# Maxima products of an attention kernel taken from the placed tiles, in the full tile shape, one head behind the other

## The chip, the cores and the metric

The kernel runs on one core of a Trainium2 chip. The metric is the device time of one execution, in microseconds (us). The kernel before takes 3608.76 us (median of three runs, 3608.7 to 3609.93 us). Engines are called by their profile names: PE (TensorE), PEld (its weight loads), DVE (VectorE), ACT (ScalarE), POOL (GpSimd), and SP (SyncE), which here only issues DMA transfers; SPq is its queue in the rows.

## The reference, cut to what matters

The input is x of shape (8, 1024, 256). After a layer norm, the result is x + attention(xn) + mixture-of-experts(xn). The attention has 16 heads of width 64:

```
q = xn @ Wq.T + bq ; k = xn @ Wk.T + bk ; v = xn @ Wv.T + bv      (8 batches, 16 heads, 1024, 64)
att = softmax(q @ k.T / 8)                                         (1024 x 1024 for each batch and head)
out = (att @ v) @ Wo.T + bo
```

The experts (64 of width 192, 8 chosen for each token) take their turns beside the attention. All is computed to float32 accuracy. Where a product runs in the one-pass format of float32 (`F32R`), its operands are split into a rounded "high" part and a "low" rest, and products of the parts are added up.

## The kernel before, in words

Four stages follow one another: layer norm and values (`norm_stage`), a small table of token counts (`table_stage`), attention together with experts (`attention_stage`), and the output projection (`output_stage`). The change is in the third.

The attention stage works on pairs of heads: 8 batches by 8 pairs make NP = 64 pairs. `run_steps` runs steps s = -2 to 64. In step s the kernel finishes pair s-1 (`fin`), computes scores, exponentials and values products of pair s (`att`), computes the maxima of pair s+1 (`nxt`), projects queries and keys of pair s+2 (`prj`), and works on one expert. Steps 3 to 60 are a hardware loop, two steps an iteration; the others are written out.

**How a pair moves through the tiles.** The projection (`PJ`, L974) leaves queries and keys in PSUM. ACT writes their rounded high part into `high` (L1033), DVE the rest into `low` (L1107). In both tiles the two heads of a pair lie on partitions 0 to 63 and 64 to 127. Scores want another layout, so SP copies them, from SBUF to SBUF, with 12 transfers a pair (`SHUFFLES`), which are called the placement here: for each head, `k_full` holds the high keys twice (top and bottom 64 partitions), `q_full` the high queries on top of the low queries, `k_rest` the low keys, and `q_rest` the high queries. They increment the semaphore `placed` (16 each, 192 a pair). In step s SP issues the placement of pair s+1 once three things have come about: all four low parts of that pair (`lows_ready`), the placement before, and the last exponential of step s-1 (`probs_ready`, since the buffers to be overwritten were read by the scores of that pair). On SP's queue the placement stands behind the store of the second half's output of step s-1 (`store`, L1269) and the load of half of the projection's input for a later pair (`load_tokens`, L777, 1 MB); behind it come the row of maxima (L1261), the next expert's weights (L1301 to L1306), the next values (L1315), projection weights, the other half of the input, and stores.

**Scores.** `score` writes keys by queries of one head, 128 by 512, into one of three PSUM banks, with two matmuls (L898 with 128 rows of `k_full` and `q_full`, L901 with 65 rows of `k_rest` and `q_rest`; the 65th row subtracts each query's maximum). The step's first score waits for `placed` of its own pair. ACT turns them into exponentials (L1062), POOL adds these up (L1226, L1227), PE multiplies them with the values (`pv`, L942), and `add_up` (L952) sums over keys.

**Maxima.** `quad` computes, for 128 queries of the pair s+1, both heads' products with all 1024 keys, in four PSUM banks of 512 columns (`work`): four matmuls of 64 rows each (L927), straight from `high`. They go part by part, and within a part head 0 (rows 0 to 63), then head 1 (rows 64 to 127). DVE reduces each head's two banks to a negated maximum (L1099). Each step has 8 quads. The wait at the step's first quad, `highs_ready`, is for the pair's high parts, which ACT wrote in the step before.

**The order on PE.** It is written out by hand in `step` and is the same for each of four slots g: eight scores, with a projection and an expert's or transpose's item between them; quad 2g; in slot 0 `add_up(s, 1)` and the last `pv` of pair s-1, in slot 2 `add_up(s, 0)`, in slots 1 to 3 `pv(s, g-1)`; quad 2g+1. An engine does its instructions in order, so whatever stands behind a waiting instruction waits too.

Of the kernel before, what the change touches and what calls it, by code (L numbers as in the profile page):

```python
# [25 lines left out]
P = 128  # L26
B, N, D = 8, 1024, 256
T = B * N
H, DK = 16, 64
# [11 lines left out]
HALF = 512  # L41
# [5 lines left out]
DMA = 16  # L47
# [12 lines left out]
def known(v, least):  # L60

    return isinstance(v, int) and v < least
# [628 lines left out]
SHUFFLES = 12  # L691
# [97 lines left out]
def attention_stage(nc, ctx, io, keep):  # L789
    def sb(name, shape, dt=F32):  # L790
        return ctx.enter_context(nc.sbuf_tensor(name, shape, dt))

    def sem(name):
        return ctx.enter_context(nc.semaphore(name))
# [5 lines left out]
    work = psum[:, 4:8, :]  # L800
# [3 lines left out]
    q_full = sb("q_full", [P, 2, 2, N], F32R)  # L804
    q_rest = sb("q_rest", [DK + 1, 2, 2, 2, HALF], F32R)
    k_full = sb("k_full", [P, 2, 2, N], F32R)
    k_rest = sb("k_rest", [DK + 1, 2, 2, N], F32R)

    high = sb("high", [P, 2, 2, N], F32R)
# [32 lines left out]
    highs_ready = sem("highs_ready")  # L842
    lows_ready = sem("lows_ready")
    placed = sem("placed")
    quad_filled = sem("quad_filled")
# [33 lines left out]
    def _(pe):  # L879
# [24 lines left out]
        def quad(s, par, flags, q):  # L904

            g = q // 2
            fin, att, nxt, prj = flags
            if q == 0:
                pe.wait_ge(highs_ready, 4 * (s + 2))
            if q % 2 == 0:  # L910
                if prj:
                    pe.wait_ge(lows_ready, 4 * (s + 2) + g + 1)
                if att and g == 0:
                    pe.wait_ge(xt_copied, s + 1)
                    pe.wait_ge(shift_ready[1], s + 1)
                if att and g == 1:
                    pe.wait_ge(gate_ready, s + 1)
                if g == 2:
                    pe.wait_ge(shift_ready[0], s + 2)
                if att and g == 3:  # L920
                    pe.wait_ge(y_weighted, s + 1)
            if not known(QUADS * (s + 1) + 2 * q, 1):
                pe.wait_ge(quad_reduced, QUADS * (s + 1) + 2 * q)
            for part in range(2):
                for h in range(2):
                    rows = slice(DK * h, DK * (h + 1))
                    last = nc.tensor.matmul(work[:, 2 * h + part, :], high[rows, 1 - par, 0, q * P:(q + 1) * P],  # L927
                                            high[rows, 1 - par, 1, part * HALF:(part + 1) * HALF], start=True, stop=True)
                    if part == 1:
                        last.then_inc(quad_filled, 1)  # L930

        def pv(p, par, gg):
            pe.wait_ge(probs_ready, SCORES * p + 8 * (gg + 1))
# [69 lines left out]
        def step(s, par, flags):  # L1003
            fin, att, nxt, prj = flags
            for g in range(SLOTS):
                for n in range(2 * GROUP):
                    if att:
                        score(s, par, fin, g, n // 2, n % 2)
                    if n in ITEMS[g] and present(ITEMS[g][n], g, flags):
                        item(s, par, flags, g, ITEMS[g][n])  # L1010
                if nxt:
                    quad(s, par, flags, 2 * g)
                if g == 0 and fin:
                    add_up(s, 1, fin)
                    pv(s - 1, 1 - par, SLOTS - 1)
                if g == 2 and att:
                    add_up(s, 0, fin)
                if g > 0 and att:
                    pv(s, par, g - 1)
                if nxt:  # L1020
                    quad(s, par, flags, 2 * g + 1)
# [610 lines left out]
```

## Time and profile before

| | |
|---|---|
| median of three runs | 3608.76 us |
| the profiled execution | 3610.97 us |
| its span, first to last instruction | 3609.2 us |
| mean granted PE clock | 0.984 of full |
| PE busy | 3503.0 us, 97% |
| POOL busy | 2711.3 us, 75% |
| DVE busy | 2517.0 us, 70% |
| ACT busy | 1685.6 us, 47% |
| maxima products, L927 | 2048 matmuls, 378.0 us busy |

The span is divided by stage: up to about 408 us lie the first two stages, then the attention stage up to about 3395 us, then the output stage. Busy times are of the whole span; a group of instructions by line shows its summed time without overlaps and the mean length of one, which is longer where two run at once.

### The profile page before, as it was taken

The page shows a single profiled execution, that of the slowest core. Times are in us where ns is not written, and L with a number is a line of the kernel's source. Part 1 is how long each engine was busy: PE and PEld are TensorE (multiplying, and loading weights), DVE is VectorE, ACT ScalarE, POOL GpSimd, SP SyncE. Part 2 cuts the span into 40 slices and gives each one's busy share as a digit, 9 for nine tenths or more (in the row PEclk, how much of TensorE's full clock was granted, in tenths as well). Part 3 has the DMA queues.
Part 4 walks back from the last instruction along what each step waited for, and adds up shares of the span by engine and source line. Part 5 has one row for each costly group of instructions (what it writes and reads, how often), then busy time and mean ns, then how long its engine had stood idle before and what let it go on. Part 6 is the DMA issues. An engine that isn't in the chain of part 4 may idle for free. (4 is left out here: it accounts for less than half of the span.)

```text
span 3609.2 us, 59812 instructions
## 1 busy us (share of the span) xinstructions
PE 3503.0 (97%) x16231; PEld 2104.9 (58%) x16232; DVE 2517.0 (70%) x3256; ACT 1685.6 (47%) x3126; POOL 2711.3 (75%) x2338
## 2 busy tenths in 40 slices
PE   8999489999999999999999999999999999999899
PEld 6888255555555555555555555555555555555487
DVE  7888467777777777777777777777777777777444
ACT  4455234444444444444444444444444444444343
POOL 1111168888888888888888889888888888889511
PEclk9999689999999999999999999999999999999899
DMA  7777545666666666666666666666666666665396
GB/s 249 230 227 224 150 117 137 173 168 168 169 168 170 170 168 168 170 171 169 170 169 172 168 169 169 171 167 171 168 171 168 168 169 172 169 172 130 117 320 227
DMA packets 393627, 635.53 MB, mean 176 GB/s; under 512 B 48048, under 2 KB 214640, under 8 KB 393584
## 3 DMA queue, kind: packets, MB, share of 16 engines
q1 hardware_dynamic: 370800, 603.54, 60.3%
q0 software_dynamic: 14336, 23.08, 3.1%
q10 hardware_dynamic: 8448, 8.39, 0.7%
q8 instruction: 21, 0.34, 0.0%
q14 instruction: 22, 0.18, 0.0%
HBM read 306.91 MB, written 126.12 MB: 120 GB/s over the span
## 5 line engine op out<-in xcount | busy, mean ns | idle before, releaser
L1099 DVE TENSOR_REDUCE merged<-psum 128x1 f32<-128x1024 f32 x1024 | 1206.0, 1219 | 732.9 <-PE psum L927 726.8
L1062 ACT ACTIVATE probs<-psum 128x512 f32<-128x512 f32 x2048 | 1083.3, 600 | 1160.5 <-PE psum L901 867.6
L1226 POOL TENSOR_TENSOR sums<-sums,probs 128x512 f32<-128x512 f32 x768 | 979.8, 1276 | 97.9 <-ACT probs L1062 43.4
L1227 POOL TENSOR_TENSOR sums<-sums,probs 128x512 f32<-128x512 f32 x768 | 981.1, 1277 | 0.0
L942 PE MATMUL psum<-probs,v_sb 128*64 128x512 f32 x4096 | 931.0, 596 | 0.0
L898 PE MATMUL psum<-q_full,k_full 128*128 128x512 f32 x2048 | 878.8, 429 | 0.0
L901 PE MATMUL psum<-q_rest,k_rest 65*128 65x512 f32 x2048 | 812.3, 397 | 0.0
L942 PEld LDWEIGHTS psum<-probs,v_sb 128*64 128x64 f32 x4096 | 284.0, 137 | 560.8 <-issue 498.4
L898 PEld LDWEIGHTS psum<-q_full,k_full 128*128 128x128 f32 x2048 | 388.2, 190 | 196.9 <-issue 95.2
L1127 DVE RECIPROCAL sum_all<-sum_all 128x128 f32<-128x128 f32 x512 | 448.7, 918 | 27.7 <-ACT sum_all L1070 27.7
L974 PE MATMUL psum<-x_t,w_qk 128*128 128x512 f32 x1536 | 416.3, 407 | 38.0 <-DVE w_d L1092 27.5
L901 PEld LDWEIGHTS psum<-q_rest,k_rest 65*128 65x128 f32 x2048 | 390.0, 190 | 61.5
L927 PE MATMUL psum<-high 64*128 64x512 f32 x2048 | 378.0, 446 | 18.9 <-DVE merged L1099 12.2
L974 PEld LDWEIGHTS psum<-x_t,w_qk 128*128 128x128 f32 x1536 | 282.2, 193 | 135.0 <-DVE w_d L1092 27.7
L927 PEld LDWEIGHTS psum<-high 64*128 64x128 f32 x2048 | 154.4, 186 | 324.1 <-issue 299.5
L1226 POOL TENSOR_TENSOR sums<-probs 128x512 f32<-128x512 f32 x128 | 165.5, 1293 | 174.9 <-ACT probs L1062 173.2
L1033 ACT ACTIVATE high<-psum,bias 128x512 fp32r<-128x512 f32 x256 | 176.0, 688 | 238.0 <-PE psum L974 233.2
L1107 DVE SCALAR_TENSOR_TENSOR low<-psum,bias,high 128x512 fp32r<-128x512 f32 x256 | 177.4, 693 | 28.1 <-ACT high L1033 28.1
L1527 PE MATMUL psum<-ot_sb,wo 128*128 128x512 f32 x768 | 186.7, 402 | 10.3 <-ACT ot_sb L1447 10.3
L1527 PEld LDWEIGHTS psum<-ot_sb,wo 128*128 128x128 f32 x768 | 145.7, 192 | 45.7 <-issue 11.2
L1422 POOL TENSOR_TENSOR rest<-x_out,moe_sb 128x1024 f32<-128x1024 f32 x16 | 41.2, 2575 | 165.1 <-DVE y L1484 129.7
L1227 POOL TENSOR_TENSOR sums<-probs 128x512 f32<-128x512 f32 x128 | 163.0, 1274 | 0.0
(145 smaller groups left out, 3059.8 us busy)
## 6 DMA issues: line engine op xcount, KB each, us to landing
x_t<-xt SPq DMA_DIRECT2D x118, 1024.0 KB
k_full<-high SPq DMA_DIRECT2D x256, 256.0 KB
v<-values SPq DMA_DIRECT2D x64, 512.0 KB, 3.2
w_qk<-wqk_parts SPq DMA_DIRECT2D x64, 512.0 KB
q_full<-high SPq DMA_DIRECT2D x128, 256.0 KB
q_full<-low SPq DMA_DIRECT2D x128, 256.0 KB
k_rest<-low SPq DMA_DIRECT2D x128, 256.0 KB
q_rest<-high SPq DMA_DIRECT2D x128, 256.0 KB
```

What stands on the lines that cost most here:

```text
L898: nc.tensor.matmul(out, k_full[:, par, h, keys], q_full[:, par, h, cols], start=True, stop=False)
L901: nc.tensor.matmul(out, k_rest[:, par, h, keys], q_rest[:, par, half, h, :], start=False, stop=True).then_inc(scores_ready, 1)
L927: last = nc.tensor.matmul(work[:, 2 * h + part, :], high[rows, 1 - par, 0, q * P:(q + 1) * P], high[rows, 1 - par, 1, part * HALF:(part + ...
L942: last = nc.tensor.matmul(out_ps[rows, :], v_sb[:, par, kt, rows], probs[:, kt, h, :], start=(kt == 0), stop=(kt == KT - 1))
L974: last = nc.tensor.matmul(out, w_qk[:, par, which, wp, kd, :], x_t[:, xp, kd, cols], start=(j == 0 and kd == 0), stop=(j == 2 and kd == KD ...
L1062: nc.scalar.activation(probs[:, kt, h, :], ring[ring_place(g, j) % RING], ACT.Exp, scale=SCALE).then_inc(probs_ready, 1)
L1099: nc.vector.tensor_reduce(out=merged[:, col:col + 1], in_=work[:, 2 * h:2 * h + 2, :].rearrange("p b c -> p (b c)"), axis=AX, op=ALU.max, ...
L1107: nc.vector.scalar_tensor_tensor(out=low[:, par, which, cols], in0=work[:, 0, :], scalar=bias[:, par, which:which + 1], in1=f32(high[:, pa ...
L1127: nc.vector.reciprocal(sum_all[:, half, cols], sum_all[:, half, cols]).then_inc(recip_ready, 1)
L1226: nc.gpsimd.tensor_tensor(sums[:, half, 0, :], first[:, 0, :], probs[:, kt, 0, :], ALU.add)
L1227: nc.gpsimd.tensor_tensor(sums[:, half, 1, :], first[:, 1, :], probs[:, kt, 1, :], ALU.add).then_inc(sums_added, 1)
L1527: last = nc.tensor.matmul(psum[:, 2 * par + c, :], wo[:, t, h, c * P:(c + 1) * P], ot[:, par, o, h, :], start=(n == 0), stop=(n == 3 * PAI ...
```

## The change

Two edits, both in `quad`:

```diff
             if q == 0:
-                pe.wait_ge(highs_ready, 4 * (s + 2))
+                pe.wait_ge(placed, DMA * SHUFFLES * (s + 2))
...
-            for part in range(2):
-                for h in range(2):
-                    rows = slice(DK * h, DK * (h + 1))
-                    last = nc.tensor.matmul(work[:, 2 * h + part, :], high[rows, 1 - par, 0, q * P:(q + 1) * P],
-                                            high[rows, 1 - par, 1, part * HALF:(part + 1) * HALF], start=True, stop=True)
-                    if part == 1:
-                        last.then_inc(quad_filled, 1)
+            for h in range(2):
+                for part in range(2):
+                    last = nc.tensor.matmul(work[:, 2 * h + part, :], q_full[:, 1 - par, h, q * P:(q + 1) * P],
+                                            k_full[:, 1 - par, h, part * HALF:(part + 1) * HALF], start=True, stop=True)
+                last.then_inc(quad_filled, 1)
```

The four products of a quad read `q_full` and `k_full`, 128 rows each, in place of 64 rows of `high`; a product is then (high + low queries) by high keys. Head 0's two parts come first, then head 1's, and DVE is told of a head after its second matmul: after matmuls 2 and 4, where it was after 3 and 4. The first quad of step s waits for the placement of pair s+1, which SP issues in the same step, in place of the high parts that were ready in the step before.

## Rows read from the trace of the kernel before

**Rows 1.** The page: busy us of each engine, share of the span, instructions
```profile
PE 3503.0 (97%) x16231; PEld 2104.9 (58%) x16232; DVE 2517.0 (70%) x3256; ACT 1685.6 (47%) x3126; POOL 2711.3 (75%) x2338
```
**Rows 2.** Windows of the loop's stage: length, each engine's busy us (instructions), clock, DMA share, GB/s
```profile
524.00:3300.00 2776.00, 2775.53 (x12894) 1553.00 (x12889) 1978.05 (x2313) 1334.59 (x2612) 2465.20 (x2129) 1.00 0.64 168
```
**Rows 3.** Timeline of PE, one step: start, us, instruction, count; quad 0 first and last
```profile
1799.25 0.73 PE L927 MATMUL psum<-high 64*128 64x512 f32 x4
...
1844.91 0.73 PE L927 MATMUL psum<-high 64*128 64x512 f32 x4
```
**Rows 4.** Timeline of PE, a quad between a score and pv, and scores behind another
```profile
1811.37 0.40 PE L901 MATMUL psum<-q_rest,k_rest 65*128 65x512 f32 x1
1811.70 0.73 PE L927 MATMUL psum<-high 64*128 64x512 f32 x4
1812.37 3.65 PE L942 MATMUL psum<-probs,v_sb 128*64 128x512 f32 x16
...
1816.61 0.50 PE L898 MATMUL psum<-q_full,k_full 128*128 128x512 f32 x1
1816.95 0.40 PE L901 MATMUL psum<-q_rest,k_rest 65*128 65x512 f32 x1
1817.19 0.40 PE L898 MATMUL psum<-q_full,k_full 128*128 128x512 f32 x1
```
**Rows 5.** Waits in the whole span: who for whom, us in total, times, longest
```profile
DVE merged L1099 <- PE psum L927: 726.8, 506, 3.4
```
**Rows 6.** Timeline of ACT: the last two exponentials of a step
```profile
1833.85 1.08 ACT L1062 ACTIVATE probs<-psum 128x512 f32<-128x512 f32 x2
```
**Rows 7.** Timeline of SP in that step: issues of the input, the placement, the weights
```profile
1834.13 0.62 SPq L777 DMA_DIRECT2D x_t<-xt  x1
1835.03 1.17 SPq L1289 DMA_DIRECT2D k_full<-high  x2
...
1849.33 1.28 SPq L1290 DMA_DIRECT2D q_rest<-high  x1
...
1851.77 0.40 SPq L1301 DMA_DIRECT2D w_gu<-in_w_gu  x1
```
**Rows 8.** Window over the placement's transfers, columns as in rows 2
```profile
1836.00:1855.00 19.00, 19.00 (x90) 10.63 (x87) 12.84 (x15) 8.42 (x17) 17.07 (x15) 1.00 1.04 238
```
**Rows 9.** DMA issues, 1834 to 1860 us: KB each, us from issue to landing
```profile
w_gu<-in_w_gu SPq DMA_DIRECT2D x1, 384.0 KB, 5.0
```
**Rows 10.** DMA issues, 1800 to 1900 us: a store of 256 KB
```profile
ot<-out_raw SPq DMA_DIRECT2D x4, 256.0 KB, 2.0
```
**Rows 11.** Timeline of PE at the stage's head, with the idle time before and its releaser
```profile
430.94 1.22 PE L927 MATMUL psum<-high 64*128 64x512 f32 x4 [1.66 <-DVE low L1107]
...
437.20 2.90 PE L974 MATMUL psum<-x_t,w_qk 128*128 128x512 f32 x6 [1.40 <-DVE merged L1099]
...
477.57 0.84 PE L927 MATMUL psum<-high 64*128 64x512 f32 x4 [2.41 <-DVE merged L1099]
...
478.94 0.63 PE L901 MATMUL psum<-q_rest,k_rest 65*128 65x512 f32 x1
```
**Rows 12.** Windows of 0.5 us there: PE busy (instructions), clock, DMA share, GB/s
```profile
440.50:441.00 0.50, 0.00 (x0) 0.99 0.84 172
...
478.00:478.50 0.50, 0.50 (x5) 0.56 0.76 169
...
484.50:485.00 0.50, 0.50 (x3) 0.61 0.00 0
```
**Rows 13.** SP at the head and in step 1: first issue of a placement without an input load
```profile
426.39 1.18 SPq L1289 DMA_DIRECT2D k_full<-high  x2
...
511.12 1.16 SPq L1289 DMA_DIRECT2D k_full<-high  x2
```
**Rows 14.** Window of 2 us in the head's placement, columns as in rows 2
```profile
430.00:432.00 2.00, 1.06 (x4) 0.53 (x4) 0.75 (x1) 0.01 (x1) 0.00 (x0) 0.50 0.99 201
```
**Rows 15.** Timeline of PE, quad 0 of step 1
```profile
520.98 0.73 PE L927 MATMUL psum<-high 64*128 64x512 f32 x4
```

## The prediction

> **What bounds the kernel now.** Read the page first: PE is busy for 97% of the span, POOL for 75, DVE for 70 [rows 1]. Shares of a whole span mix stages, so the next view is the window over the attention loop: 2775.53 of 2776.00 us of PE are busy, at the full granted clock [rows 2]. There PE is the bound without a gap, and a step takes what its instructions take: quad 0 starts at 1799.25 and again at 1844.91, 45.66 us later [rows 3]. Everything else has slack; DVE waits 726.8 us for the maxima products, 1.4 us a time [rows 5]. So whatever is added to PE's order, as work or as a wait, goes into the time in full, 64 times (steps -1 to 62 have quads), and what DVE gains does not.
>
> **The wait.** In the step of the rows, the last score's exponential ends at 1833.85 + 1.08 = 1834.93 [rows 6]. SP issues 1 MB of input at 1834.13, then, from 1835.03 on, the 12 placement transfers; the last goes out at 1849.33 and is issued by 1850.61 [rows 7]. PE reaches quad 0 at 1844.91 [rows 3]. Even the issuing ends 5.7 us behind it, so the new wait stalls PE in every step, and the price is set by the landing. No row has that landing; it is bounded from both sides.
> - From below: a 256 KB store on a quiet queue lands 2.0 us after its issue [rows 10]; from 1850.61 that gives 1852.6.
> - From above: the expert's weights, issued at 1851.77 right behind, land 5.0 us later [rows 7, 9]; the same lag from 1850.61 gives 1855.6.
> - By bytes: 19 us at 238 GB/s from 1836 to 1855 are 4.52 MB [rows 8]. The input (1.05), twelve times 0.262 (3.15) and POOL's gather and scatter (0.20) make 4.39 MB, so the placement ends close to 1855. The weights say the same: landed at 1856.8, and 0.39 MB at this rate take 1.6 us, so they begin at 1855.1.
>
> I take 1855.0, since two ways meet there. PE would come to quad 0 not at 1844.91 but 0.4 us later (quads 6 and 7, which lie between the last exponential's scores and quad 0, get dearer, below). The stall is 1855.0 - 1845.3 = 9.7 us; by the bounds 7.3 to 10.3.
>
> Does it recur in full? Yes: the placement starts at the last exponential of the step before, and from there to quad 0 PE's path is fixed, so the distance is the same each time; time lost behind quad 0 delays the next exponential and with it the next placement. What is queued behind quad 0 on PE is `add_up`, the last `pv` of the pair before, and all scores; ACT, DVE and POOL stand behind these, so nothing is done in the stall that would be saved later. On SP the next values' load waits for that `pv`, and now goes out after it, about when it would anyway, a step before its use: nothing. The DMA engines are full during the placement (share 1.04 in rows 8), so it can't be expected to shorten.
>
> **The matmuls.** Now a quad lasts from its start to the next instruction 1812.37 - 1811.70 = 0.67 us for four matmuls [rows 4]. Full-shape matmuls of 512 columns follow one another at 1817.19 - 1816.95 = 0.24 us. But the shape changes cost something now: from the score to the quad 1811.37 to 1811.70 = 0.33, and the first score behind a quad takes 1816.61 to 1816.95 = 0.34, each 0.10 over the 0.24. A full-shape quad with `pv` on one side and scores on the other: 4 x 0.24 = 0.96 for 0.67, less one border of 0.10, so +0.2 us. Bounds: none of the border comes back, +0.3; both borders come back, +0.1. There are 8 quads a step, of which two hide in the stall (subtracted there): 8 x 0.2 = 1.6 us (0.8 to 2.4). The earlier signal for head 0 (after matmul 2) is worth nothing while DVE waits for PE; the second is later by the 0.3 us of the quad, under DVE's mean wait of 1.4 us.
>
> The Trainium skill bears on this ("TensorEngine Tiling (Array Packing)", Key Properties): a change of tiling mode drains TensorE, while differing tiles compute in parallel. The first half speaks for the change, the second against it. The borders of 0.33 and 0.34 us and the two overlapping matmuls of a pair show both; by the drain alone the edit would gain 0.1 us a quad, and with the parallelism lost it costs 0.2.
>
> **The clock.** The stall has a second price. At the stage's head PE idles 2.41 us before 477.57; at 478.0 to 478.5 the granted clock falls to half (1.2 GHz), and full (2.4) is back at about 484.7 [rows 11, 12]. The score matmul at 478.94 takes 0.63 us there, where the same one takes 0.40 at full clock [rows 11, 4]. Four times in the head PE came to work with the clock already at half; in three of them full clock returned 3.3 us after the start of the work (as 437.20 to 440.5, rows 11 and 12), in the fourth later, but within 6 us. A stall of 9.7 us is longer than any of those gaps, so PE will come out of it at half clock, for 3.3 to 6.6 us (440.5 - 437.20 and 484.7 - 478.1); half of that is lost: 1.6 to 3.3 us. I take 2.5, the middle. With no drop it would be 0.
>
> The skill's "TensorE: Matmul & The Clock Gate", HAM oscillation, tells of this pattern: a loop whose iterations each wait on a DMA pays the return to full clock every time. The rows at the head agree in kind (1.2 GHz after idling 2.41 us); whether it comes back in this loop no row of before can show.
>
> **Sum.** A step of the loop: 9.7 + 1.6 + 2.5 = 13.8 us. Input loads precede the placement in steps 4 to 61, 58 steps: 800 us. In steps 1, 2, 3 and 62 there is no such load. The placement alone is 3.15 MB at 0.2 MB/us [rows 14], 15.7 us, with 0.9 us beside the data (2.0 us for the store of rows 10, less 0.262 MB at the 0.238 of rows 8): in step 1, 511.12 + 16.6 = 527.7, against quad 0 at 520.98 + 0.4 [rows 13, 15], a stall of 6.3; with 1.6 and 2.5 that is 10.4 us, four times 42 us. Step -1: 426.39 + 16.6 = 443.0 against 430.94 [rows 11, 13], 12.1 us, and 1.5 for dearer quads at half clock: 14. Step 0: its placement waits for low parts and not for exponentials; by the same reckoning about 4.5 of stall, 1.6 and 1.5 more: 8. Together 800 + 42 + 22 = 864 us. The profiled execution took 3610.97 us, 1.8 us over its span, 2.2 us over the median. 3610.97 + 864 = 4475; in terms of the median, **4473 us**. A step of the loop would last 59.5 us.
>
> **The rivals.**
> 1. *The stall comes, the clock stays.* Then 64 x 2.5 = 160 us less: 4313. For it: the fall at 478 came in one particular head, with sparse work before. Against: the clock also fell to half in the head's other gaps, all shorter than 9.7 us.
> 2. *The clock recovers late.* If, instead of 3.3 to 6.6, some 12 us go at half clock in each step, 3.5 us more are lost: +224, 4697. For it: a step that stalls regularly has less activity than any stretch of the loop before. Against: after every gap in the head it was full again within 7.2 us of the work's start.
> 3. *The wait is hidden, only the matmuls count.* 512 quads at 0.2: +102, 3711. It wants the placement landed by 1845.3, 10 us after its first issue. Against: SP issues until 1850.61.
> 4. *Not slower: the full shape gains.* One mechanism: no change of shape around quads any more. If a full-shape quad cost no more than the 0.67 us of now, the two borders would give back 0.2 us x 512 = 102 us: 3507. It decides only if the 64-row pairs do not really run side by side (four matmuls spaced 0.24 would fall to 0.17), and if the landing comes before PE is at quad 0. The rows of scores at 0.24 and rows 7 are against both.
> 5. *The edit does not do what it says*: were `placed` already at its count at quad 0, because the counts refer to an earlier pair. Then the time would be rival 3's. They don't: 192 x (s+2) is pair s+1's, the one issued in this step.
>
> **From there to the numbers.** The forecast 0.84, rival 1 0.06, rival 2 0.04, rival 3 0.03, rival 4 0.01 and the rest 0.02 (among it no change). The forecast's own ends: a step of 7.3 + 0.8 + 1.6 = 9.7 to 10.3 + 2.4 + 3.3 = 16.0 us, so +610 to +1010 us; the low end needs three extremes at once. The range reaches from 4290, which takes in rival 1, to 4620. A difference of 0.2% (7 us) is about what a measurement of this kernel can tell; slower by more than that has 0.97, within it 0.01, faster 0.02.
>
> **What would show it right or wrong.** In the profile after: PE's share falls to about 83% (49.8 of 59.5 us in a step), with an idle time of about 9.7 us ahead of the first matmul of quad 0 in each step, released by a DMA or unexplained; quad 0 to quad 0 59.5 us; a granted clock of 0.50 for some us behind it, and a mean over the loop of about 0.90 (5 us of work and some 6 of the stall at half, of 59.5); L927 at 0.24 us from matmul to matmul. Steps of 47 us without gaps would mean the placement had landed; steps of 57 with the clock at 1.00, rival 1; steps over 62, rival 2 or a placement that got slower.

## The result and the profile after

| | before | after |
|---|---|---|
| median | 3608.78 us (4 runs) | 4554.1 us (4 runs, 4548.15 to 4558.06) |
| ratio, 95% interval | | 1.2617 [1.2595, 1.2639] |
| profiled execution, span | 3610.97, 3609.2 us | 4558.06, 4556.3 us |
| mean granted PE clock | 0.984 | 0.902 |
| L927 (L926 after), PE busy | 378.0 us | 663.0 us |

The change costs 945 us, where 864 were forecast. Lines behind `quad` stand two lower after the change, in `quad` one. The page's busy times answer to [rows 1], the window over the loop to [rows 2]:

```profile
PE 3806.6 (84%) x16232; PEld 2387.3 (52%) x16232; DVE 2534.6 (56%) x3256; ACT 1685.6 (37%) x3126; POOL 2710.8 (59%) x2338
```
```profile
524.00:4300.00 3776.00, 3142.22 (x13207) 1865.27 (x13206) 2047.19 (x2366) 1369.68 (x2682) 2530.59 (x2186) 0.90 0.49 125
```

PE was busy without a gap in this stage; now 634 of its 3776 us are idle, and the clock is 0.90. The busy time of ACT and POOL is what it was, that of DVE 18 us more in 2517: the other engines have hardly more work. The waits (who for whom, us in total, times, longest) name the reason; the DVE row answers to [rows 5]:

```profile
PE psum L926 <- DMA q_rest<-high: 651.5, 64, 14.7
DVE merged L1097 <- PE psum L926: 1580.1, 512, 14.4
```

64 waits, one for each step with quads, all released by the last transfer of the placement. They make up 651.5 of the 945 us. One of them, in SP's timeline, which answers to [rows 7]:

```profile
1978.04 0.62 SPq L777 DMA_DIRECT2D x_t<-xt  x1
1979.52 1.16 SPq L1287 DMA_DIRECT2D k_full<-high  x2
...
1993.08 1.29 SPq L1288 DMA_DIRECT2D q_rest<-high  x1
```

and in PE's, quad 0 first, then `add_up`, `pv` and quad 1 (idle time and its releaser in brackets):

```profile
1999.33 2.05 PE L926 MATMUL psum<-k_full,q_full 128*128 128x512 f32 x4 [9.69 <-DMA q_rest<-high]
2001.31 1.98 PE L950 MATMUL psum<-sums,ones 128*64 128x512 f32 x4
2003.07 4.86 PE L940 MATMUL psum<-probs,v_sb 128*64 128x512 f32 x16
2007.86 1.20 PE L926 MATMUL psum<-k_full,q_full 128*128 128x512 f32 x4
```

The last transfer is issued by 1994.37 and lands 5.0 us later. The reader should also see what follows the wait: `add_up` takes 2003.07 - 2001.31 = 1.76 us to the next line. The same three pieces in slot 2 of the step before, without a wait in front:

```profile
1965.62 1.08 PE L926 MATMUL psum<-k_full,q_full 128*128 128x512 f32 x4
1966.64 1.08 PE L950 MATMUL psum<-sums,ones 128*64 128x512 f32 x4
1967.55 3.60 PE L940 MATMUL psum<-probs,v_sb 128*64 128x512 f32 x16
1971.08 1.20 PE L926 MATMUL psum<-k_full,q_full 128*128 128x512 f32 x4
```

From quad to next quad 8.53 us behind the wait, 5.46 without: 3.07 us are lost to the clock in this step (2.65 in the next). These two lie above the mean: over all 61 waits of the loop it is 7.86 us from quad 0 to quad 1 (6.90 to 8.59), where 5.54 pass at full clock (so in `e3_shape_only`, below), so 2.3 us a step. Windows of 1 us show it (PE busy, clock, DMA share, GB/s), as [rows 12] did at the head: the clock falls at 1992, in the wait, and is full again at 2005.5, 6 us after the work has started.

```profile
1990.00:1991.00 1.00, 0.00 (x0) 1.00 1.04 252
1992.00:1993.00 1.00, 0.00 (x0) 0.50 1.02 225
1999.00:2000.00 1.00, 0.67 (x2) 0.50 0.64 213
2004.00:2005.00 1.00, 1.00 (x6) 0.50 0.00 0
2005.00:2006.00 1.00, 1.00 (x4) 0.70 0.00 0
2006.00:2007.00 1.00, 1.00 (x8) 1.00 0.00 0
```

The quads themselves, between a score and `pv`, and between `pv` and scores; these answer to [rows 4]:

```profile
1977.88 0.39 PE L901 MATMUL psum<-q_rest,k_rest 65*128 65x512 f32 x1
1978.28 1.18 PE L926 MATMUL psum<-k_full,q_full 128*128 128x512 f32 x4
1979.39 3.65 PE L940 MATMUL psum<-probs,v_sb 128*64 128x512 f32 x16
1982.98 1.20 PE L926 MATMUL psum<-k_full,q_full 128*128 128x512 f32 x4
1984.01 0.39 PE L898 MATMUL psum<-q_full,k_full 128*128 128x512 f32 x1
1984.24 0.40 PE L901 MATMUL psum<-q_rest,k_rest 65*128 65x512 f32 x1
```

From score to `pv` it is now 1.51 us for 1.00 before: the border in front stayed (0.40), and four matmuls take 1.11 for 0.67. That first border is not the same at every quad. In slot 2, where `add_up` follows, it is gone (1965.62 - 1965.39 = 0.23 us, before 0.33):

```profile
1965.39 0.39 PE L901 MATMUL psum<-q_rest,k_rest 65*128 65x512 f32 x1
```

In front of the quads that `pv` follows, it varies from 0.24 to 0.44 us. From quad to the second matmul of the scores, 1.26 for 1.00: four take 1.03, and the 0.10 of the border behind them is gone (0.23).

The loop's step, from quad 0 to quad 0 over 54 steps, is (4191.05 - 903.84)/54 = 60.9 us, against 45.66 before [rows 3]; the forecast had 59.5:

```profile
903.84 2.05 PE L926 MATMUL psum<-k_full,q_full 128*128 128x512 f32 x4 [9.68 <-DMA q_rest<-high]
```
```profile
4191.05 2.07 PE L926 MATMUL psum<-k_full,q_full 128*128 128x512 f32 x4 [9.55 <-DMA q_rest<-high]
```

### The profile page after: what moved, and what is told of

It reads as the page before. It is cut to its first block and busy times, and to the rows that moved or that the text cites. A ratio compares the mean times of both kernels' runs of the same rounds, so it can differ in the third digit from the quotient of the medians.

```text
span 4556.3 us, 59813 instructions
## 1 busy us (share of the span) xinstructions
PE 3806.6 (84%) x16232; PEld 2387.3 (52%) x16232; DVE 2534.6 (56%) x3256; ACT 1685.6 (37%) x3126; POOL 2710.8 (59%) x2338
## 5 line engine op out<-in xcount | busy, mean ns | idle before, releaser
L926 PE MATMUL psum<-k_full,q_full 128*128 128x512 f32 x2048 | 663.0, 449 | 666.0 <-DMA q_rest<-high 651.5
L940 PE MATMUL psum<-probs,v_sb 128*64 128x512 f32 x4096 | 969.9, 617 | 0.0
L926 PEld LDWEIGHTS psum<-k_full,q_full 128*128 128x128 f32 x2048 | 384.5, 206 | 1004.1 <-issue 871.2
L898 PE MATMUL psum<-q_full,k_full 128*128 128x512 f32 x2048 | 851.3, 416 | 0.0
L940 PEld LDWEIGHTS psum<-probs,v_sb 128*64 128x64 f32 x4096 | 298.4, 145 | 627.3 <-issue 580.9
L1068 ACT COPY sum_all<-psum 128x512 f32<-128x512 f32 x128 | 74.9, 585 | 920.8 <-PE psum L950 920.8
L972 PEld LDWEIGHTS psum<-x_t,w_qk 128*128 128x128 f32 x1536 | 294.6, 192 | 109.0 <-DVE w_d L1090 27.6
L1224 POOL TENSOR_TENSOR sums<-probs 128x512 f32<-128x512 f32 x128 | 164.7, 1287 | 220.0 <-ACT probs L1060 213.2
L1105 DVE SCALAR_TENSOR_TENSOR low<-psum,bias,high 128x512 fp32r<-128x512 f32 x256 | 189.6, 741 | 27.4 <-ACT high L1031 27.4
L950 PE MATMUL psum<-sums,ones 128*64 128x512 f32 x512 | 190.6, 833 | 3.6 <-POOL sums L1225 3.6
```

The lines of the kernel that those rows point to most:

```text
L898: nc.tensor.matmul(out, k_full[:, par, h, keys], q_full[:, par, h, cols], start=True, stop=False)
L926: last = nc.tensor.matmul(work[:, 2 * h + part, :], q_full[:, 1 - par, h, q * P:(q + 1) * P], k_full[:, 1 - par, h, part * HALF:(part + 1) ...
L940: last = nc.tensor.matmul(out_ps[rows, :], v_sb[:, par, kt, rows], probs[:, kt, h, :], start=(kt == 0), stop=(kt == KT - 1))
L950: last = nc.tensor.matmul(ring[place % RING][DK * h:DK * (h + 1), :], ones[:], sums[:, half, h, :], start=True, stop=True)
L972: last = nc.tensor.matmul(out, w_qk[:, par, which, wp, kd, :], x_t[:, xp, kd, cols], start=(j == 0 and kd == 0), stop=(j == 2 and kd == KD ...
L1224: nc.gpsimd.tensor_tensor(sums[:, half, 0, :], first[:, 0, :], probs[:, kt, 0, :], ALU.add)
```

## The experiments

**The wait alone** (`e1_wait_only`), from the kernel before:

```diff
             if q == 0:
-                pe.wait_ge(highs_ready, 4 * (s + 2))
+                pe.wait_ge(placed, DMA * SHUFFLES * (s + 2))
```

> The kernel before with the new wait alone: the first quad of a step waits for its pair's placement, the products stay the 64-row pairs from the high parts. My theory: the wait is nearly all of the loss. In the changed kernel a step waits 10.2 us in the mean and loses about 2.9 us to the half clock; here quads 0 to 5, which lie behind the wait, are each 0.25 to 0.5 us shorter (1.85 us a step), and quads 6 and 7, which lie in front of it, only lengthen the wait by 0.7 us. So 4554 - 64 x 1.85 = about 4436 us, stalls of about 11 us in each step. Rival (the dearer products and the change of shapes around them are what costs, the wait is partly made up elsewhere): under 4100 us.

Measured: 4448.64 us, 1.2325 [1.2301, 1.2349] of before. PE's waits, and the products at their old cost:

```profile
PE psum L927 <- DMA q_rest<-high: 697.8, 64, 14.9
```

The wait brings 840 of the 945 us: 698 as idle time, the other 142 (2.2 us a step) with the clock, whose mean over the loop is 0.90 here too. From quad 0 to quad 1 it is 7.28 us here in the mean of the loop, for 5.10 before: the same 2.2. The idle time is 46 us longer than after the whole change, 0.7 us a step; there two dearer quads stand ahead of the wait, and by the lines above they cost 0.51 and 0.26 us more.

**The products alone** (`e3_shape_only`), with the old wait, and for that reason from other data: 128 rows of the high parts, so a product is the sum over both heads. The edit against the changed kernel, beside the old wait:

```diff
             for h in range(2):
                 for part in range(2):
-                    last = nc.tensor.matmul(work[:, 2 * h + part, :], q_full[:, 1 - par, h, q * P:(q + 1) * P],
-                                            k_full[:, 1 - par, h, part * HALF:(part + 1) * HALF], start=True, stop=True)
+                    last = nc.tensor.matmul(work[:, 2 * h + part, :], high[:, 1 - par, 0, q * P:(q + 1) * P],
+                                            high[:, 1 - par, 1, part * HALF:(part + 1) * HALF], start=True, stop=True)
```

> The kernel before with full-shape products, one head behind the other, but read from the high parts (128 rows of both heads, so each product is the sum over both heads; the maxima are of that sum) and with the old wait. Theory: the products' share of the change by itself, 8 quads a step with 0.25 us more each in front of scores and 0.5 us more in front of values products: 512 x 0.33 = 170 us, 3780 us, PE busy without a gap and the clock full. By the forecast's term (0.2 us a quad) it would be 3711 us. Rival (no changes of shape around quads, hence no loss): 3609 us or less.

Measured: 3759.3 us, 1.0419 [1.0398, 1.0439]; PE busy for 2774.29 us of the window of 2776 and the clock full. 151 us over 512 quads are 0.295 us each; a step of the loop takes 48.14 us for 45.66, 0.31 a quad. The two halves of the change add up to 840 + 151 = 991; less the 46 us that are hidden in the wait, that is the 945.

**The order alone** (`e2_order_only`): the 64-row products as before, head 0's two first.

```diff
-            for part in range(2):
-                for h in range(2):
+            for h in range(2):
+                for part in range(2):
...
-                    if part == 1:
-                        last.then_inc(quad_filled, 1)
+                last.then_inc(quad_filled, 1)
```

> The kernel before with the order of the four products alone: head 0's two parts, then head 1's, still 64 rows each from the high parts, old wait. Theory (products on different row halves run side by side, so order matters as much as shape): matmuls on the same rows follow one another at about 0.24 us, a quad takes 0.95 to 1.05 instead of 0.67 us, and the time is 3609 + 512 x 0.3 = about 3770 us. Rival (only the full shape costs, order is free, or the earlier signal to the reducing engine helps): 3605 to 3620 us.

Measured: 3608.42 us, 1.0001 [0.999, 1.0011]. My theory fell: order costs nothing. A quad between `pv` and scores:

```profile
1847.29 0.74 PE L927 MATMUL psum<-high 64*128 64x512 f32 x4
1847.96 0.50 PE L898 MATMUL psum<-q_full,k_full 128*128 128x512 f32 x1
```

It still takes 0.67 us. So either 64 rows are fast by themselves, or the pairs form whatever the order. The next two ask that.

**One half of the rows** (`e8_same_rows`): all four products from rows 0 to 63.

```diff
-                    rows = slice(DK * h, DK * (h + 1))
+                    rows = slice(0, DK)
```

> The kernel before with all four 64-row products of a quad read from rows 0 to 63 (the second head's maxima are then the first head's), same order and wait. e2_order_only took no time, which fits two readings. Theory (the halves of the rows work side by side, and in e2 the second head's products were started beside the first head's although they stand behind them): with one half only, four products go one behind the other at 0.235 us, a quad takes 0.95 to 1.0 us, and the time is 3609 + 512 x 0.3 = about 3760 us, as e3_shape_only. Rival (64 rows are fast by themselves, the other half has nothing to do with it): 3605 to 3615 us.

Measured: 3828.55 us, 1.0612 [1.0591, 1.0633]:

```profile
1824.95 1.20 PE L927 MATMUL psum<-high 64*128 64x512 f32 x4
1826.07 0.50 PE L898 MATMUL psum<-q_full,k_full 128*128 128x512 f32 x1
1826.41 0.39 PE L901 MATMUL psum<-q_rest,k_rest 65*128 65x512 f32 x1
```

A quad takes 1.12 us for 0.67, and here both borders stay as well (0.34 behind it). The rival is out: the saving of the kernel before lies in the two halves working side by side. The starts in the traces say so directly. In the kernel before, the four products of this kind of quad start at 0, 0.003, 0.337 and 0.340 us, so two at a time; in this run one by one, 0.23 to 0.34 us apart. 220 us over 512 quads are 0.43 each; I had expected 0.3, the figure of the full shape, which gets rid of one border. Four 64-row products on one half are dearer than four of 128 rows.

**A fence between the heads** (`e9_order_fenced`): e2 with a wait, long met, in front of head 1's first product.

```diff
             for h in range(2):
+                if h:
+                    pe.wait_ge(lows_ready, 4 * (s + 2))
                 for part in range(2):
```

> e2_order_only with a wait that has long been met between the first head's two products and the second head's. Theory (in e2 a product of the second head is started ahead of one of the first head on its own half of the rows): if the wait holds the second head back until the queue reaches it, the first head's two products go one behind the other, a quad takes about 0.95 us, and the time is about 3740 to 3770 us. Rival (the start order has nothing to do with the queue's order or was changed when the program was compiled, and such a wait stops nothing): 3605 to 3620 us.

Measured: 3607.98 us, 0.9999 [0.9989, 1.0009]. It stops nothing. The records of the trace show what runs: the product that carries this wait, head 1's first, starts 0.007 us behind head 0's first, and head 0's second only 0.33 us later, although it stands ahead in the kernel. In e2, too, the two that start last are the ones that signal DVE, one of each head. So between products on different halves of the rows, the order of starts is not that of the kernel. Whether head 1's product overtakes on the engine or was put in pairs when the program was compiled is left open.

**The engine kept at work** (`e4_warm`): the changed kernel with the old wait first, 36 matmuls whose result quad 0 overwrites, and then the new wait.

```diff
+            if q == 0:
+                for _ in range(36):
+                    nc.tensor.matmul(work[:, 0, :], high[:, 1 - par, 0, 0:P], high[:, 1 - par, 1, 0:HALF],
+                                     start=True, stop=True)
+                pe.wait_ge(placed, DMA * SHUFFLES * (s + 2))
```

> The changed kernel with 36 more full-shape matmuls ahead of the wait for the placement in each step, on data that is ready, their result overwritten by quad 0. They take 36 x 0.236 = 8.5 us of a stall of 10.2 us, so PE works through it. Theory (the half clock behind the stall is a cost of its own, 2.9 us a step): the clock stays full, the step loses only the wait, 4554 - 64 x 2.9 = about 4370 us. Rival (the clock's fall costs nothing, since the matmuls behind it wait for something else): 4554 us; if the stall has more to do with contention by PE's reads, more than 4554 us.

Measured: 4426.97 us, 1.2271 [1.2247, 1.2295] of before, 127 us under the changed kernel, with 36 matmuls more a step. A stall:

```profile
1707.60 8.43 PE L926 MATMUL psum<-high 128*128 128x512 f32 x36
1717.58 1.19 PE L931 MATMUL psum<-k_full,q_full 128*128 128x512 f32 x4 [1.56 <-DMA q_rest<-high]
1718.70 1.08 PE L955 MATMUL psum<-sums,ones 128*64 128x512 f32 x4
```

Quad 0 is at 1.12 us again, and the clock of the loop is 0.99 for 0.90. Useless work makes the kernel faster. The gain is 2.0 us a step, not the 2.9 that I had taken from two steps: the mean loss is 2.3 (above), and some of it is left here, since PE still idles for 1.8 us in the mean of the loop and then needs 5.98 us from quad 0 to quad 1, for 5.54 at full clock.

**Less in front of the landing.** `e5_split` sends the eight transfers into `k_full` and `q_full` first, with a semaphore of their own for which the quads wait; `e6_late` loads the input's second half behind the next step's placement; `e7_split_late` does both.

```diff
-                pe.wait_ge(placed, DMA * SHUFFLES * (s + 2))
+                pe.wait_ge(placed_full, DMA * FULLS * (s + 2))
...
-                        sp.dma_start(f32(dst[to, pp, h, :]), f32(src[rows, pp, which, :])).then_inc(placed, DMA)
+                        sp.dma_start(f32(dst[to, pp, h, :]), f32(src[rows, pp, which, :])).then_inc(placed_full, DMA)
```
```diff
-            if loads:
-                alone(sp, (standing, 1), (lows_ready, 4 * (s + 2) + 4), (x_loaded[1], DMA * x_loads(s + 2)))
-                load_tokens(sp, io, keep, s + 3, 1)
...
+            if not known(s, LOOP0) and not (isinstance(s, int) and s > NP - 3):
+                alone(sp, (standing, 1), (lows_ready, 4 * (s + 1) + 4), (x_loaded[1], DMA * late_loads(s + 1)))
+                sp.dma_start(...)     # input of pair s+2, second half
```

> The changed kernel with the placement reordered and its signal divided: the eight transfers into the two tiles that the quads read go first and have a semaphore of their own, the quads wait for these only; the four others follow. Theory (the landing is a matter of bytes in front of it: 1.05 MB of input and 3.15 MB of placement at 0.2 to 0.24 MB a us): 1.05 MB less, the wait shrinks by 4.4 to 5.2 us to some 5.5 us; the clock still falls. 4554 - 64 x 4.8 = about 4250 us. Rival (a fixed delay of the transfers' completion, not bytes, or the queue's issuing): a wait shorter by less than 2 us, above 4430 us.

> The changed kernel with the second half of the projection's input (1 MB) loaded behind the placement of the next step instead of ahead of it. Theory (bytes in front): the input's 1.05 MB go at 0.3 to 0.35 MB a us, so 3 to 4 us less wait in 58 steps; 4554 - 58 x 3.5 = about 4350 us, and the stalls of the loop then are like those of the steps that never had such a load (7.2 to 8.8 us). Rival (the placement's rate is set by its own packets and the input overlaps with it): above 4480 us.

> Both: quads wait for the first eight transfers, and no input load goes ahead of the placement. Theory: 2.1 MB at 0.2 MB a us and 1.5 us beside the data land some 12 us behind the first issue, the wait is 2 us or less; with so short an idle time the clock may stay full in most steps, and then the 2.9 us go too: 4554 - 64 x (10.2 - 2 + 2.9) = about 3850 us, of which some 170 are the dearer products. With the clock still falling: about 4030 us. Rival (landing is not a matter of bytes): above 4300 us.

| | us | of before, 95% | PE idle for the placement |
|---|---|---|---|
| e5_split | 4234.49 | 1.1735 [1.1712, 1.1758] | 343.1 us |
| e6_late | 4392.56 | 1.2166 [1.2142, 1.219] | 510.7 us |
| e7_split_late | 3997.36 | 1.1071 [1.1049, 1.1093] | 160.5 us |

Each from its own waits:

```profile
PE psum L929 <- DMA q_full<-low: 343.1, 63, 10.4
```
```profile
PE psum L931 <- DMA q_rest<-high: 510.7, 64, 15.7
```
```profile
PE psum L934 <- DMA q_full<-low: 160.5, 63, 10.4
```

Four transfers fewer (1.05 MB) take 308 us off, 4.8 a step, as expected. By itself this does not tell bytes from issues, since four issues of 1.1 to 1.3 us go too. What speaks for bytes: the first issues of a placement without an input load in front take only some 0.6 us each, and the later 1.3, which is 0.262 MB at 0.2 MB a us; and `e6_late`, where one short issue goes (0.62 us), saves 2.4 us:

```profile
3215.19 0.62 SPq L1296 DMA_DIRECT2D q_full<-high  x1
3215.85 1.30 SPq L1296 DMA_DIRECT2D q_full<-low  x1
```

The input's 1.05 MB give only 141 us of idle time, 2.4 us in each of 58 steps and not 3.5. In the changed kernel its issue is 1.5 us ahead of the placement's (1978.04 and 1979.52), so that part of it has moved by then; how much is not shown. With both, some 2.4 us of wait are left, and the total is 147 us over the expectation. Two steps of the loop show most of the rest, quad 0 with its successor, and the windows behind:

```profile
3226.73 2.05 PE L934 MATMUL psum<-k_full,q_full 128*128 128x512 f32 x4 [2.27 <-DMA q_full<-low]
3228.71 1.56 PE L958 MATMUL psum<-sums,ones 128*64 128x512 f32 x4
```
```profile
3278.68 1.16 PE L934 MATMUL psum<-k_full,q_full 128*128 128x512 f32 x4 [2.39 <-DMA q_full<-low]
3279.77 1.08 PE L958 MATMUL psum<-sums,ones 128*64 128x512 f32 x4
```
```profile
3228.00:3230.00 2.00, 2.00 (x6) 0.57 1.01 196
...
3280.00:3282.00 2.00, 2.00 (x12) 1.00 1.02 194
```

After the same idle time the clock is at half in the one step and full in the other; they last 51.95 (3226.73 to 3278.68) and 50.5 us. Of the loop's 60 waits, 19 leave the clock full, behind 2.06 to 2.75 us of idle time, and 41 do not, behind 2.10 to 3.91 us. The mean loss is 1.25 us a step, some 80 us in all, where the expectation had the clock stay full in most steps and took back 2.9 us in each. None of these comes near the kernel before; the experiments point to no version that beats it.

## Why the prediction was right

The time (4554) lies in the range and the mechanism is the one forecast. By its own steps, for a step of the loop:

| term | forecast | measured | from |
|---|---|---|---|
| the step before | 45.66 | 45.66 | [rows 3] |
| stall for the placement | 9.7 | 10.2 | 651.5 us over 64 waits |
| dearer quads, 8 of them | 1.6 | 2.4 to 2.5 | 151 us / 512 x 8, and the loop's step, e3 |
| half clock behind the stall | 2.5 | 2.3 | quad 0 to quad 1, mean of 61 waits; e1: 2.2, e4: 2.0 |
| the step after | 59.5 | 60.9 | 54 steps |

The measured terms add up to 60.6 to 60.7; the remaining 0.2 to 0.3 us have no term here. The forecast was 81 us too low. Two terms were too small, the waiting by 47 us and the matmuls by 49, and one was too large, the clock by some 13 (64 x 0.2); together 83. The total owes little to luck.

**The wait.** Right in kind, place and size, and e1 shows it alone. The landing was 5.0 us behind the end of issuing, the bound from above; I took 4.4. Over 64 steps the idle time is 651.5 us where the forecast's stalls add up to 58 x 9.7 + 4 x 6.3 + 12.1 + 4.5 = 604. That the distance is the same each time did not hold: the waits of the loop last from 7.9 to 11.7 us, with a mean of 10.2. No run asks what makes them differ.

**The matmuls.** The term that was mis-sized most: 0.295 us a quad and not 0.2, 49 us in all. 4 x 0.24 was taken from matmuls in the middle of a run of them. The four starts of one quad, read one by one in PE's timeline, with `pv` at 1979.39 behind:

```profile
1978.28 0.49 PE L926 MATMUL psum<-k_full,q_full 128*128 128x512 f32 x1
...
1978.61 0.40 PE L926 MATMUL psum<-k_full,q_full 128*128 128x512 f32 x1
...
1978.84 0.39 PE L926 MATMUL psum<-k_full,q_full 128*128 128x512 f32 x1
...
1979.07 0.39 PE L926 MATMUL psum<-k_full,q_full 128*128 128x512 f32 x1
```

They are 0.33, 0.23, 0.23 and 0.32 apart: the first and the last spacing are longer. The first stands between two products of one shape; behind the last the shape does change, to the 128*64 of `pv`, so the full shape does not remove that border. What comes back is the border between a quad and the scores behind it, and the one in front of the quads in slot 2; at the quads that `pv` follows nothing does. I had credited 0.10 to every quad. The bound from above, 0.3, just about held (0.295 over all, 0.31 in the loop). The reason given, that the 64-row products work side by side, is shown by e8. What the reading of the code suggested, that the alternating order is what pairs them, is false by e2.

**The clock.** Right. The profile after shows half clock behind the waits, and e4 that the price is one of its own, 2.0 to 2.3 us a step.

**The rivals.** No clock loss: out by the profile after and e4. Late recovery: out, the clock is full 6 us after the start of the work, and no step of the loop needs more than 8.59 us from quad 0 to quad 1. The argument against it had a hole, though. It said that after every gap in the head the clock was full again within 7.2 us of the work's start; but from 415 to 440 us it stayed at half throughout, over several pieces of work of up to 2.9 us (PE busy, clock, DMA share, GB/s):

```profile
415.00:440.00 25.00, 14.84 (x34) 0.50 0.57 125
```

There gaps of 1.6 us and more stood between the pieces; behind the stall the work has none. A hidden wait: out, all 64 wait. A gain by the full shape: out by e3. The edit doing nothing: out.

## What to carry to other kernels

A wait moved from "the data is computed" to "the copy has landed" costs the distance between its landing and the waiting instruction in every iteration; where the waiting engine is the bound, read both times from one step's timelines, and bound the landing by the bytes queued in front of it. Add the clock: behind stalls of 8 to 12 us, PE lost 2.3 us more here. And a product over half of the rows is not half wasted when its neighbour uses the other half: filling the array with the full shape made four products dearer, 1.03 to 1.11 us for 0.67.

## What the runs showed of the hardware that was not expected

The order of four 64-row products on two halves of the rows makes no difference (3608.42 for 3608.38 us), not even with a met wait between the halves (3607.98): one of each half start together, against the order in the kernel. And an idle time of 2.1 to 2.7 us sends the clock to half in some steps and not in others of the same loop (`e7_split_late`, 19 of 60 kept it full).
